# Four-layer graph network: when batches are gathered, root products made and transposed x kept

## The reference

```
seg    = dst * 16 + edge_type
summed = segment_sum(x[src], seg)              # 6250*16 rows of 128
cnt    = segment_sum(1, seg)
agg    = summed / max(cnt, 1)
out    = einsum('nrd,rdh->nh', agg, W1) + x @ root1 + b1
x1     = relu(out)                             # then the same again with W2, root2, b2
```

## Time and profile before

| | us |
|---|---|
| median of 3 runs | 5924.92 |
| lowest and highest run | 5918.19 and 5926.52 |
| span of the profiled execution | 5914.8 |

### The profile page before, as it was taken

How to read it: one execution, slowest core, us unless ns; L and a number is a source line. 1 busy time by engine, 2 the same in 40 slices (tenths; PEclk the granted TensorE clock), 3 DMA queues, 4 the chain that set the end, 5 groups by cost and what they waited for, 6 DMA issues and landing times. The chain is left out here.

```text
span 5914.8 us, 110361 instructions
## 1 busy us (share of the span) xinstructions
PE 4223.3 (71%) x25432; PEld 3507.0 (59%) x25433; DVE 2686.0 (45%) x10126; ACT 1772.9 (30%) x5020; POOL 4151.1 (70%) x4271
## 2 busy tenths in 40 slices
PE   5688878878777777466666667666666657877786
PEld 3577777767777776455555555555555545555554
DVE  8743434343333332465656566445544552224222
ACT  0122222222222222344444445444444430002001
POOL 3177777757777776477777773777777757776777
PEclk6699999999999999565656567888888889888898
DMA  3266656542211111233333332233232344444443
GB/s 84 59 171 157 155 160 159 154 129 53 52 52 52 52 53 50 65 83 83 83 83 83 83 80 57 87 99 99 87 99 87 99 134 142 136 146 126 147 136 106
DMA packets 383068, 594.88 MB, mean 101 GB/s; under 512 B 120483, under 2 KB 289988, under 8 KB 372420
## 3 DMA queue, kind: packets, MB, share of 16 engines
q0 software_dynamic: 133120, 276.30, 17.9%
q1 hardware_dynamic: 245156, 310.79, 17.8%
q10 hardware_dynamic: 4128, 1.75, 0.1%
HBM read 519.07 MB, written 69.42 MB: 99 GB/s over the span
## 5 line engine op out<-in xcount | busy, mean ns | idle before, releaser
L1418 PE MATMUL PS<-ROOM 128*128 128x128 f32 x8320 | 1046.0, 283 | 130.7 <-ACT ROOM L1019 99.3
L1418 PEld LDWEIGHTS PS<-ROOM 128*128 128x128 f32 x8320 | 987.0, 196 | 190.0 <-ACT ROOM L1019 108.1
L846 POOL DMA_INDIRECT GB<-table,IDX x832 | 805.5, 968 | 316.9 <-issue 252.9
L1019 ACT COPY ROOM<-PS 128x512 f32<-128x512 f32 x1040 | 609.3, 586 | 1020.8 <-PE PS L1432 1019.4
L846 POOL DMA_INDIRECT GB<-in_x,IDX x416 | 404.8, 973 | 294.7 <-ACT IDX L993 158.0
L1432 PE MATMUL PS<-OH,GB 128*128 128x256 f32 (+1 forms) x1664 | 367.8, 384 | 242.3 <-DMA GB<-table,IDX 189.0
L2083 DVE TENSOR_TENSOR ROOM<-ROOM,PS 128x128 f32 x312 | 89.7, 287 | 988.7 <-PE PS L1442 981.2
L806 POOL DMA_INDIRECT GB<-table_gat,IDX x416 | 430.3, 1034 | 127.6 <-issue 126.5
L818 POOL DMA_INDIRECT GB<-table,IDX x416 | 395.5, 951 | 173.2 <-issue 125.6
L806 POOL DMA_INDIRECT H<-table_gat,IDX x416 | 423.1, 1017 | 126.8 <-issue 125.2
L846 POOL DMA_INDIRECT ROOM<-table,IDX x416 | 409.0, 983 | 126.8 <-issue 125.6
(11 more groups left out here) (415 smaller groups left out, 7964.1 us busy)
## 6 DMA issues: line engine op xcount, KB each, us to landing
H<-one_over SPq DMA_DIRECT2D x416, 128.0 KB
ROOM<-one_over SPq DMA_DIRECT2D x416, 128.0 KB
neighbours<-ROOM SPq DMA_DIRECT2D x26, 1700.0 KB
ROOM<-neighbours SPq DMA_DIRECT2D x26, 1700.0 KB
PACK<-neighbours SPq DMA_DIRECT2D x26, 1700.0 KB
ROOM<-local_row SPq DMA_DIRECT2D x104, 256.0 KB, 3.4
GB<-table,IDX POOLq DMA_INDIRECT x1248
ROOM<-table,IDX POOLq DMA_INDIRECT x832
```

What stands on the lines that cost most here:

```text
L846: pool.indirect_dma_start(out=r.rows[c][:, j * P:(j + 1) * P], out_offset=None, in_=r.dram[:, :], in_offset=bass.IndirectOffsetOnAxis(ap=I ...
L1019: act.copy(to.rearrange("p r (j d) -> p r j d", j=r.per), of.rearrange("p (j d r) -> p r j d", j=r.per, d=NEAR))\
L1418: ins = nc.tensor.matmul(PS[:, 4, 0:P], r.near[1 - b][:, t * P:(t + 1) * P], r.weights[:, t * P:(t + 1) * P], start=t == 0, stop=t == r.re ...
```

## The change

- POOL gathers ten batches (`EARLY`) instead of four before the round, taking indices from `idx1` (`gather_early`). Batches 0 to 3 go to the four slots as before. Batches 4 to 9 go into columns 0 to 6143 of `X`, which then hold no x any more. Before batch 4 POOL waits until these columns are stored in a new DRAM tensor `x_turned` (3072 KB, stored by SP behind its other stores) and until all 16 root products are made.
- Therefore the root products of x are no longer made after the count, but one in each of the count's first 16 iterations of two batches, between the sum of the first and that of the second batch. Each is in bank 0 and waits until ACT has taken the one before. PE waits for all weights before the count.
- ACT stages the index lists of batches 10 to 13 at the end of steps 0 to 3, none in steps 4 to 9, and that of k + 4 from step 10 on. Batch 10 goes to slot 0, and so on.
- Steps 0 to 11 are written out instead of steps 0 to 3. After step 11, ACT loads `X`'s columns back from `x_turned` (3072 KB), and DVE waits for that before line 2129.
- The semaphores of batches 4 to 9 are those of later rounds, whose wait values are raised to match.

```
+EARLY = 10
+        x_turned = nc.dram_tensor("x_turned", [P, (EARLY - 4) * G * P], FP32, kind="Internal").ap()
...
+            def rows_of(self, k, c):
+
+                if isinstance(k, int) and k in self.early:
+                    return self.rows[k] if k < FOUR else X[:, (k - FOUR) * G * P:(k - FOUR + 1) * G * P]
+                return self.rows[(c - self.turn) % FOUR]
...
+            sp.wait_ge(turn_a, N_COLS // 2 + N_XG)
+            sp.wait_ge(base_in, 96)
+            sp.dma_start(x_turned, X[:, 0:(EARLY - FOUR) * G * P]).then_inc(base_in, 16)
             sp.wait_ge(degree, 3)
...
+            def gather_early(r):
+
+                pool.wait_ge(turn_sb, 1)
+                for k in r.early:
+                    if k == FOUR:
+                        pool.wait_ge(base_in, 96 + 16)
+                        pool.wait_ge(ground_ps, CHUNKS)
+                    for j in range(G):
+                        pool.indirect_dma_start(
+                            out=r.rows_of(k, k % FOUR)[:, j * P:(j + 1) * P], out_offset=None, in_=r.dram[:, :],
+                            in_offset=bass.IndirectOffsetOnAxis(ap=idx1[:, k * G + j:k * G + j + 1], axis=0),
+                        ).then_inc(early_in[k], 16)
...
-                    if now < BATCHES - FOUR:
+                    if isinstance(k, int) and k < len(r.early):
+                        if k < FOUR:
+                            stage(k + EARLY, (k + EARLY) % FOUR)
+                    elif now < BATCHES - FOUR:
                         stage(k + FOUR, c)
...
+                if parts[0][0] > 1:
+                    act.dma_start(X[:, 0:(EARLY - FOUR) * G * P], x_turned).then_inc(w_in, 16)
...
-            act.wait_ge(turn_sb, 1)
-            for c in range(FOUR):
-                stage(c, c)
+            act.sem_inc(near_idx, EARLY)
...
-            sum_round(count)
+            pe.wait_ge(w_in, 16 * N_W_IN)
+
+            def root_chunk(i, b, low):
+
+                if b == 0 and low == 0:
+                    pe.wait_ge(ground_sb, i)
+                    nc.tensor.matmul(PS[:, 0, 0:CHUNK], mat("L0_gnn_root1"), X[:, bass.ds(i * CHUNK, CHUNK)],
+                                     start=True, stop=True).then_inc(ground_ps, 1)
+
+            sum_round(count, ((0, CHUNKS), (CHUNKS, BATCHES // 2)), root_chunk)
...
-            pe.wait_ge(w_in, 16 * N_W_IN)
-            for c in range(CHUNKS):
-                if c >= 4:
-                    pe.wait_ge(ground_sb, c - 3)
-                nc.tensor.matmul(PS[:, c % 4, 0:CHUNK], mat("L0_gnn_root1"), X[:, c * CHUNK:(c + 1) * CHUNK],
-                                 start=True, stop=True).then_inc(ground_ps, 1)
...
+            dve.wait_ge(w_in, 16 * N_W_IN + 16)
             for g in range(GROUPS):
                 dve.wait_ge(root_ps, g + 1)
```

More of the change, by code:

```diff
@@ L448, in __init__ @@
                 self.g0, self.d0, self.q0 = n * SPARSE, n * DENSE, n * XBLOCKS
-                self.landed = [n * (16 * G) * len(range(c, SPARSE, RING)) for c in range(RING)]
+                self.landed = [16 * G + n * (16 * G) * len(range(c, SPARSE, RING)) for c in range(RING)]
         D_TILE, P_TILE = 10 + 2 * FINE + 2, FINE + 2
@@ L503, in build @@
         x2_stored, pads = sem("x2_stored"), sem("pads")
+        early_in = near_in + mx_in + r_gat.gathered[0:EARLY - 2 * FOUR]
+        EARLY_GAT = [16 * G * (c < EARLY - 2 * FOUR) for c in range(FOUR)]
         def counted_steps(steps):
@@ new lines, in gather_near, with one @@
+            def gather_near(r):
+                def one(k, c):
+                    pool.wait_ge(near_idx, k + (r.first + 1))
+                    pool.sem_inc(near_passed, 1)
+                    for j in range(G):
+                        pool.indirect_dma_start(
+                            out=r.rows_of(k, c)[:, j * P:(j + 1) * P], out_offset=None, in_=r.dram[:, :],
+                            in_offset=bass.IndirectOffsetOnAxis(ap=IDX[:, c, j:j + 1], axis=0),
+                        ).then_inc(near_in[(c - r.turn) % FOUR], 16)
+                early = len(r.early)
+                whole = -(-early // FOUR)
+                for k in range(early, whole * FOUR):
+                    one(k, k % FOUR)
+                with pool.Fori(whole, BATCHES // FOUR) as i:
+                    for c in range(FOUR):
+                        one(FOUR * i + c, c)
@@ L1029, in run_near @@
             def run_near(step, parts=((1, BATCHES // FOUR - 1),), ground=None):
-                for c in range(FOUR):
-                    step(0, c)
+                for k in range(parts[0][0] * FOUR):
+                    step(k // FOUR, k % FOUR)
+                if parts[0][0] > 1:
+                    act.dma_start(X[:, 0:(EARLY - FOUR) * G * P], x_turned).then_inc(w_in, 16)
                 for low, high in parts:
@@ L1065, in _ @@
             act.wait_ge(over_out, 16)
-            run_near(step)
+            run_near(step, ((near_a.unrolled, BATCHES // FOUR - 1),))
             for g in range(GROUPS):
@@ L2019, in wide @@
                         dve.wait_ge(slow_p, theirs)
-                        step(dve.tensor_copy(S_ROWS[:, :], r.rows[c][:, bass.ds(j * P, P)]))
+                        step(dve.tensor_copy(S_ROWS[:, :], r.rows_of(k, c)[:, bass.ds(j * P, P)]))
                         if r.looks:
@@ L2102, in near_round @@
                     dve.tensor_copy(wcol[:, 0:G], wstage[:, 0, :]).then_inc(w_added, 1)
-                for c in range(FOUR):
-                    step(0, c)
-                low = 1
+                for k in range(r.unrolled * FOUR):
+                    step(k // FOUR, k % FOUR)
+                low = r.unrolled
                 if mix:
```

37 lines of the change are left out of this document (20 added, 17 removed).

## The result

The changed kernel takes **5884.49 us** (median of 4 runs, 5883.55 to 5904.12) beside 5925.72 us of the kernel before (4 runs): 0.9942 of its time, 95% interval 0.993 to 0.9954. I go by "25 to 41".

A forecast was written before the change was run, and what follows sets the result against it. POOL's gathers were taken to bound the first round at 10.06 us a batch. The terms -20.6 + 5 + 1 + 1 made -13.6 us, so 5901.2 from the profiled 5914.8, plus 10.1: 5911.3 us, range 5902 to 5926.

The forecast's parts named there:

- ten batches at PE's pace: First round: ten batches pass at PE's 8.00 us a batch instead of POOL's 10.06, gaining 20.6 us.
- root products in the count: Count's first 16 iterations: a root product each, partly hidden in PE's 0.69 us between sums; +5 us, ends 0 and 21.
- store of x_turned: Count: SP's store is an instruction of about half a microsecond in a queue that next waits at 240; cost 0.
- first step at a lower clock: Start of the round: PE idles longer before step 0, whose products may run at half clock; +1 us, between 0 and 2.
- load back: After step 11: loading X back takes 7.9 us, sharing the engines with windows and gathers; +1 us, ends 0 and 8.
- written-out steps: First round: eight more written-out steps run at the loop's pace; 0, between -1 and 2 us.
- D: Count: the early batches aren't there in time, each of the six late costing up to 10.06 us; chance 3%.
- E: Count: the 48 added gathers hold DVE, costing 23.5 us, so +9.9 in all, 5935 us; chance 2%.
- A: First round: all six batches are saved, 60 us less the same 7, giving 5872 us; chance 2%.
- Rival C: Count: PE becomes its bound, 1.68 us in each of 16 iterations, +8.3 in all, 5933 us; chance 7%.
- the strict case: Load back: window packets wait behind the load's in strict turns, costing 8 us and putting the forecast 7 us higher.
- the base: Whole kernel: the runs' median lies 10.1 us above the profiled span of 5914.8, added to the forecast.

The follow-up runs named there:

- roots_in_count_only: The changed kernel with four early batches, no store or load back, root products in the count and twelve steps written out: 5908.90 us, ratio 0.9986 to the kernel before.
- roots_in_count_loop: The changed kernel with four early batches, no store or load back, and steps 4 to 11 back in the loop: 5922.40 us, 1.0005 of the kernel before.
- u_dve: The kernel before with steps 0 to 11 written out on VectorE alone: 5898.80 us, ratio 0.9965.
- five_early: The changed kernel with five early batches instead of ten, so one in X and a store of 512 KB: 5898.59 us, 0.9969 of the kernel before.
- ring_of_ten: The changed kernel with its ten places used in turn until batch 33, 36 steps written out and a later load back: 5848.89 us, 0.9875 of the kernel before.
- before_again: The kernel before, unchanged, measured again for a second profile: 5919.80 us, ratio 1.0002.

## Why the prediction was wrong, step by step

| step | predicted us | measured us | from |
|---|---|---|---|
| ten batches at PE's pace | -20.6 | -21.0 | first gather of the round to that of batch 14: 79.69 against 100.70 before |
| root products in the count | +5 | +0.7 | transposes in roots_in_count_only 228.22, in before 227.48 |
| store of x_turned | 0 | +5.1 | after 233.28 against 228.22 |
| first step at a lower clock | +1 | +1.1 | transposes to step 0's copy: 39.30 against 38.20; granted clock 0.60 from 262 to 273.6, 0.65 in before from 256 to 266 |
| load back | +1 | 0 | POOL isn't idle after 353.28 |
| written-out steps | 0, -1 to 2 | -13.5 to -19 | roots_in_count_loop to roots_in_count_only; u_dve, 5917.77 to 5898.80 |

**The step that failed** is, in its words, "Eight more written-out steps: steps 0 to 3 were written out before and run at the loop's pace. 0, between -1 and 2." I looked at what the written-out steps cost where they run, and there I found 0. I didn't ask what their code does to everything behind it in the same program. It moves VectorE's attention loop, and that was worth as much as the whole mechanism I had worked out: 13.5 to 19 us. Without that term the measured rest adds up to -14.1, forecast -13.6: batch 14 begins at 353.28 instead of 367.39. That the two terms came this near is in part luck, as the count below shows. With 13.5 to 19 us for the written-out steps the sum is 28 to 33, between the 25 and 41 measured. That fits but is no proof: the profiled executions of after have a stage of 1096 and 1100, 7 to 11 us shorter than before's, and not 1086.

**Right: ten batches.** The idle time of 39.74 us, ended by ACT's index copy, and 79.70 us from step 0 to step 10 (80.0 forecast). The early gathers were done at 190.8 (193 forecast), and behind the store the count went at 185 instructions in 40 us against 184. Rivals D and E are out, and A with POOL's idle time there.

**Right sum by two errors: the count.** The forecast +5 was met with +5.8, but not by what I said. The root products cost next to nothing: in roots_in_count_only the granted clock is 1.00 up to 108 us, a product takes 0.94 us and hides in PE's wait for DVE, and an iteration stays at 3.48 us. I had the product's price from the wrong row: 0.67 us is ACT's copy (10.00 us for 15), while PE's own row gives 12.40 / 16 = 0.78; it measured 0.94 at full clock and 1.70 at half. By my own figures PE's share would have risen to (2.03 + 1.33) / 3.48 = 97% at half clock, not 85%.

What cost 5 us is the store of x_turned, which I had counted as half a microsecond in SP's queue. Issued at 50.65, it holds the DMA engines at 0.96 and 369 GB/s until about 59. Beside it PE does 15 instructions in 5 us against 28 without, and DVE has idle times of 1.1 and 1.4 us that the profile calls `issue`. What is held up can be seen at the line that loads each batch's flag and base from `meta` into registers, which isn't counted as busy. From 49 to 59 us, of after and of roots_in_count_only (x count: ns shortest/median/longest):

```profile
L611 DVEq TENSOR_LOAD <-meta x4: 1709/1809/1912, 49.3 to 58.6; - x4
```

```profile
L610 DVEq TENSOR_LOAD <-meta x5: 526/532/1517, 49.2 to 57.2; - x5
```

At 0.53 us the load hides behind DVE's one-hot of 1.22 us; at 1.7 to 1.9 it doesn't, and the addition behind it comes late. DVE's one-hots of four batches thus take 12.09 us (49.24 to 61.33) where roots_in_count_only takes 7.96: 4.1 of the 5 us. Another 0.7 is lost at one batch near 66, at half clock; from then on the pace is the same. PE's own loads take up to 1.0 us instead of 0.30 beside the store. A DMA's price isn't its issue. five_early bears it out: with a sixth of the store, over at once, its loads from 52 us on take 0.53. Why a register load takes longer while the DMA engines are full, no run shows. Rival C is out, since the product is hidden.

**Right: the load back.** It was issued at 359.77. It took 16.7 us to land, not 7.9. The next windows' issues took 7.92 and 8.83 us instead of 4.03 (SP's queue in after), and DVE waited 10.23 us for one of them, PE 2.19 for DVE; POOL had four batches to gather and noticed nothing.

```profile
357.16 7.92 SPq L701 DMA_DIRECT2D H<-one_over  x8
366.09 8.83 SPq L701 DMA_DIRECT2D ROOM<-one_over  x8
```

The queues' packets from 366 to 370 us (packets, MB, share): q10 carries the load, in packets of 24 KB, and q1 the windows, in packets of 1 KB.

```profile
q10 hardware_dynamic: 59, 1.45, 85.9%
q1 hardware_dynamic: 68, 0.07, 6.3%
```

This agrees with the turn by packets of the Trainium skill (DMA: Bandwidth & Descriptors, "Queues, rings and completion order"): about as many packets of each, and so twenty times the bytes for the load. The windows are held up for nearly as long as the load lasts, as I had said for the strict case. It cost nothing because the stage goes by POOL.

**Wrong: the base.** I put the runs' median 10.1 us above the span. A run's time is its span and 1.8 to 2.2 us more (after's 5902.3 and 5904.12, ring_of_ten's 5860.3 and 5862.25); the 5914.8 I worked from was simply a quick execution. So the 10.1 was a spread between executions and not something that lies around the span, though adding it was right for comparing medians. And an execution can differ from the next by 20 us (after's 5883.55 and 5904.12). A part of that is POOL's time per gather: 1.257 us in the round of before, 1.260 in that of after, and 4160 gathers go one after the other. But before_again has 1.261 in that round, so this is not the change's doing.

**Range and chances.** The range's lower end allowed for no gain in a stage that the change doesn't touch. With a spread of 20 us between executions of one kernel, 5902 was too near.

## What to carry to other kernels

- Code that is written out (or only present) in an engine's program moves everything behind it. Where another stage runs two engines on shared ports at a critical phase, that was worth about 0.3% here; test a small gain with dead code of several sizes before crediting a mechanism. One size isn't enough: two of the three tried did nothing.
- Price a bulk DMA by what runs beside it for its bytes, not by its issue, and look at register loads beside it, which no busy time shows. In the count 3072 KB cost 5 us, behind a POOL-bound stage nothing.
- More buffers pay by how long the bound engine can run ahead with them: used once they gave 14 us, used in turn until batch 33 they ended the round 41 to 43 us earlier still.

## What the runs showed of the hardware

- VectorE has idle times of 0.24 to 0.45 us at fixed lines of a loop that no semaphore explains. They move with the loop's place in the program, also when nothing more is executed. A packet of kind `instruction` starts 0.4 to 0.9 us behind each of the 47 ahead of L2284 in before. No run shows which distance brings the same pattern back.
- In the attention stage a gather lasts 0.94 us, or over 1.3 when it starts shortly behind one of VectorE's long instructions. With 80 to 88 long ones of 832 the stage takes 1105 to 1110 us, with 54 to 56 it takes 1084 to 1087. In between their number alone doesn't order the stages: 75 to 79 go with 1096 to 1101 us, 63 to 65 with 1096 to 1103.
- During a store at 369 GB/s, VectorE's register load from `meta` takes 1.7 to 1.9 us instead of 0.53, PE's up to 1.0 instead of 0.30.
- Beside a load in packets of 24 KB, a queue of 1 KB packets got about one packet for each of the load's (68 to 59 in 4 us), and so 0.07 MB against 1.45.
